# A decoder layer on one core: the layernorms' 16-bit rounded parts written by ACT instead of POOL

## The reference

```
x = x + attn(layernorm(x))           # 16 heads of 64, causal mask, w_qkv, w_out
x = x + xattn(layernorm(x), ctx)     # q, k from ctx (512 features); softmax(q k^T) mixes the features of x
x = x + ffn(layernorm(x))            # 8 experts: gate by score, best expert's low-rank update, bias
layernorm(x) = (x - mean(x)) / sqrt(var(x) + 1e-5)
```

## Time and profile before

| | us |
|---|---|
| median of 3 runs | 2772.9 (2771.0 to 2775.31) |
| the profiled execution, its own time | 2772.5 |
| its span in the trace | 2770.6 |
| PE busy | 2404.3 (87%) |
| DVE busy | 1884.6 (68%) |
| ACT busy | 782.0 (28%) |
| POOL busy | 717.5 (26%) |

### The profile page before, as it was taken

How to read it: one execution, slowest core, us unless ns; L and a number is a source line. 1 busy time by engine, 2 the same in 40 slices (tenths; PEclk the granted TensorE clock), 3 DMA queues, 4 the chain that set the end, 5 groups by cost and what they waited for, 6 DMA issues and landing times.

```text
span 2770.6 us, 37859 instructions
## 1 busy us (share of the span) xinstructions
PE 2404.3 (87%) x14389; PEld 1186.3 (43%) x14389; DVE 1884.6 (68%) x3421; ACT 782.0 (28%) x1557; POOL 717.5 (26%) x981
## 2 busy tenths in 40 slices
PE   0588888689898999869998999969989999986997
PEld 0233444344454444444444444434444444434544
DVE  4577887646876767755786777764696777764566
ACT  1033333321213333322212333431221333332110
POOL 3122433213402222212421222221330222221220
PEclk9899999899999999979999999989999999998997
DMA  6678787856746776775753777774773677776543
GB/s 177 216 174 182 161 214 179 189 140 145 146 108 126 141 151 135 140 181 129 147 125 100 150 139 143 146 186 109 158 147 106 117 149 146 143 154 159 107 76 91
DMA packets 986009, 403.97 MB, mean 146 GB/s; under 512 B 937116, under 2 KB 946332, under 8 KB 985828
## 3 DMA queue, kind: packets, MB, share of 16 engines
q1 hardware_dynamic: 985828, 401.56, 65.8%
HBM read 133.05 MB, written 33.55 MB: 60 GB/s over the span
## 4 chain that ended last, share of the span: by engine, by line
PE 59%; DVE 19%; DMA 10%; issue 6%; ACT 3%; POOL 2%; SPq 1%; ACTq 0%; POOLq 0%; DVEq 0%
PE ps_p L537 8%; PE ps_p L538 8%; PE ps_p L539 8%; DMA r<-pn 8%; PE ps_s L537 6%; PE ps_s L538 6%; PE ps_s L539 6%; PE ps_s L582 6%; PE ps_o L607 5%; DVE pn L816 4%; DVE peak L853 3%; ACT probs L742 2%; DVE bn L821 2%; DMA qk<-in_x 2%; PE ps_s L587 1%
## 5 line engine op out<-in xcount | busy, mean ns | idle before, releaser
L1080 POOL TENSOR_SCALAR pn<-probs,rden 128x640 f16<-128x640 f32 (+7 forms) x512 | 391.9, 778 | 1332.7 <-DVE rden L865 827.1
L742 ACT ACTIVATE probs<-ps_s,low,back 128x640 f32<-128x640 f32 (+7 forms) x512 | 421.7, 827 | 950.8 <-DVE low L856 840.1
L816 DVE SCALAR_TENSOR_TENSOR pn<-probs,rden,pn 128x640 f16<-128x640 f32 (+7 forms) x512 | 476.3, 962 | 193.1 <-POOL pn L1080 192.8
L537 PE MATMUL ps_p<-r,w 128*128 128x512 f16 x1344 | 515.1, 383 | 3.1 <-DVE qk L816 3.1
L538 PE MATMUL ps_p<-r,w 128*128 128x512 f16 x1344 | 514.2, 383 | 0.0
L539 PE MATMUL ps_p<-r,w 128*128 128x512 f16 x1344 | 513.7, 382 | 0.0
L582 PE MATMUL ps_s<-qk 64*128 64x512 f16 (+3 forms) x2304 | 239.0, 332 | 107.9 <-ACT probs L742 97.9
L853 DVE TENSOR_REDUCE peak<-ps_s 128x2 f32<-128x1280 f32 (+3 forms) x128 | 241.4, 1886 | 92.8 <-PE ps_s L587 90.3
L607 PE MATMUL ps_o<-r,vn 128*64 128x512 f16 (+3 forms) x2304 | 210.9, 339 | 39.3 <-issue 30.0
L539 PEld LDWEIGHTS ps_p<-r,w 128*128 128x128 f16 x1344 | 132.5, 99 | 162.1 <-issue 6.3
L582 PEld LDWEIGHTS ps_s<-qk 64*128 64x128 f16 x2304 | 90.0, 95 | 252.3 <-ACT probs L742 147.4
(11 more groups left out here) (167 smaller groups left out, 3554.0 us busy)
## 6 DMA issues: line engine op xcount, KB each, us to landing
w<-w_pairs SPq DMA_DIRECT2D x72, 512.0 KB, 4.0
qk<-in_x SPq DMA_DIRECT2D x32, 512.0 KB, 4.3
r<-wo_pairs SPq DMA_DIRECT2D x16, 1024.0 KB, 7.3
w_raw<-in_x SPq DMA_DIRECT2D x32, 512.0 KB, 4.6
out<-r SPq DMA_DIRECT2D x32, 512.0 KB, 2.9
r<-in_w_qkv SPq DMA_DIRECT2D x24, 512.0 KB, 5.8
w_raw<-in_w_qkv SPq DMA_DIRECT2D x24, 512.0 KB, 5.1
w_pairs<-w SPq DMA_DIRECT2D x24, 512.0 KB, 5.5
```

The source lines that it names most:

```text
L537: pe.matmul(ps, lh, rh, start=start and k == ks[0], stop=False)
L742: act.activation(probs_part(q, j, w), ps_s[:, j, scores(q)], ACT.Exp, bias=low[:, n % 2, i:i + 1], scale=sc, accum_out=den[:, n % 2, i:i + ...
L816: dve.scalar_tensor_tensor(out=to, in0=bank, scalar=scale, in1=rounded, op0=ALU.mult, op1=ALU.subtract).then_inc(ok, 1)
L1080: pool.tensor_scalar(to, src, scale, 1.0, ALU.mult, ALU.mult).then_inc(ok, 1)
```

## The change

The rounded part of each layernorm is no longer made by POOL from the fp32 row that ACT has written. ACT writes it itself, straight from x, by a second activation with the same scale and bias. The steps AH, LH and TH leave POOL's lists and enter ACT's: LH directly behind LX, TH behind TX, AH directly ahead of AX (which overwrites x). In each of the three layernorms that is 32 instructions, 96 in all. The waits for the buffers' release move along with them. What AX waits for is now the completion of AH, and DVE's AL waits for AX instead of AH.

```
 ACT_TAIL = """
...
-    QH3 LX0 OH1 CE0 LX1 CE1 CE2 CE3 LX2 CE4 CE5 CE6 CE7 AX0+ AX1+ AX2+ TX0 LX3 AX3+ TX1
...
+    LX0 LH0 OH1 CE0 LX1 LH1 CE1 CE2 CE3 LX2 LH2 CE4 CE5 CE6 CE7 AH0+ AX0+ AH1+ AX1+ AH2+ AX2+ TX0 TH0 LX3 LH3 AH3+
...
                     if kind == "AX":
-                        act.wait_ge(a_sh, T + 1)
+                        act.wait_ge(a_hi, T + 1)
...
+                    elif kind == "AH":
+                        act.wait_ge(a_sh, T + 1)
+                        if T >= 2:
+                            act.wait_ge(xt_in[T % 2], 16 * (T // 2))
...
+                    elif kind == "LH":
+                        if T > 0:
+                            act.wait_ge(t2_in, 16 * T)
+                        act.activation(xh2[:, 0, :], x1[:, i, :], ACT.Identity, bias=sh2[:, i:i + 1],
+                                       scale=rs2[:, i:i + 1]).then_inc(b_hi, 1)
+                    elif kind == "TH":
+                        if T > 0:
+                            act.wait_ge(t3_in, 16 * T)
+                        act.activation(xh3[:, 0, :], x1[:, i, :], ACT.Identity, bias=sh3[:, i:i + 1],
+                                       scale=rs3[:, i:i + 1]).then_inc(d_hi, 1)
...
                     elif kind == "AL":
-                        dve.wait_ge(a_hi, T + 1)
+                        dve.wait_ge(a_xn, T + 1)
```

More of the change, by code:

```diff
@@ L74 @@
 ACT_TAIL = """
-    E00 E01 CH21 E10 E11 E20 E21 KH E30 E31 JH0 OH1- E40 E41 QH0 JH1 E50 E51 OH0 E60 E61 QH1 JH2 E70 E71 QH2 JH3
-    QH3 LX0 OH1 CE0 LX1 CE1 CE2 CE3 LX2 CE4 CE5 CE6 CE7 AX0+ AX1+ AX2+ TX0 LX3 AX3+ TX1
-    LX4 AX4+ TX2 GE0 LX5 AX5+ TX3 GE1 WHI0 LX6 AX6+ TX4 GE2 WHI1 LX7 AX7+ TX5 GE3 WHI2 TX6 GE4 WHI3 TX7 GE5 WHI4
-    CH00+ CH01+ GE6 WHI5 CH10+ CH11+ GE7 WHI6 CH20+ WHI7 CH21+
+    E00 E01 CH21 E10 E11 E20 E21 KH E30 E31 JH0 OH1- E40 E41 QH0 JH1 E50 E51 OH0 E60 E61 QH1 JH2 E70 E71 QH2 JH3 QH3
+    LX0 LH0 OH1 CE0 LX1 LH1 CE1 CE2 CE3 LX2 LH2 CE4 CE5 CE6 CE7 AH0+ AX0+ AH1+ AX1+ AH2+ AX2+ TX0 TH0 LX3 LH3 AH3+
+    AX3+ TX1 TH1 LX4 LH4 AH4+ AX4+ TX2 TH2 GE0 LX5 LH5 AH5+ AX5+ TX3 TH3 GE1 WHI0 LX6 LH6 AH6+ AX6+ TX4 TH4 GE2 WHI1
+    LX7 LH7 AH7+ AX7+ TX5 TH5 GE3 WHI2 TX6 TH6 GE4 WHI3 TX7 TH7 GE5 WHI4 CH00+ CH01+ GE6 WHI5 CH10+ CH11+ GE7 WHI6
+    CH20+ WHI7 CH21+
 """
 POOL_TAIL = """
[L81 to L84, removed]
+    H00 H01 H10 H11 H20 H21 H30 H31 H40 H41 H50 H51 H60 H61 H70 H71 LS0 CHI0 LS1 CHI1 LS2 CHI2 CHI3 LS3
+    CHI4 CHI5 LS4 CHI6 LS5 CHI7 LS6 AS0+ AS1+ LS7
+    AS2+ TS0 AS3+ TS1 AS4+ TS2 AS5+ TS3 AS6+
+    TS4 AS7+ TS5 TS6 TS7
 """
@@ L102 @@
 ACT_START = """
-    AX0+ AX1+ AX2+ AX3+ AX4+ AX5+ AX6+ AX7+ CH00+ CH01+ CH10+ CH11+ CH20+ CH21+
+    AH0+ AX0+ AH1+ AX1+ AH2+ AX2+ AH3+ AX3+ AH4+ AX4+ AH5+ AX5+ AH6+ AX6+ AH7+ AX7+ CH00+ CH01+ CH10+ CH11+ CH20+
+    CH21+
 """
 POOL_START = """
-    AS0+ AS1+ AH0+ AH1+ AS2+ AH2+ AS3+ AH3+ AS4+ AH4+ AS5+ AH5+ AS6+ AH6+ AS7+ AH7+ WH0+ WH1+ WH2+ WH0++ WH1++
+    AS0+ AS1+ AS2+ AS3+ AS4+ AS5+ AS6+ AS7+ WH0+ WH1+ WH2+ WH0++ WH1++
 """
@@ L756, in rest @@
                     if kind == "AX":
-                        act.wait_ge(a_sh, T + 1)
+                        act.wait_ge(a_hi, T + 1)
                         act.activation(x_in[:, T % 2, :], x_in[:, T % 2, :], ACT.Identity, bias=sh1[:, i:i + 1],
                                        scale=rs1[:, i:i + 1]).then_inc(a_xn, 1)
+                    elif kind == "AH":
+                        act.wait_ge(a_sh, T + 1)
+                        if T >= 2:
+                            act.wait_ge(xt_in[T % 2], 16 * (T // 2))
+                        if i < 2 and b > 0:
+                            for s in range(2):
+                                act.wait_ge(at_in[s], 16 * 4 * b)
+                        act.activation(xh1[:, T % 2, 0, :], x_in[:, T % 2, :], ACT.Identity, bias=sh1[:, i:i + 1],
+                                       scale=rs1[:, i:i + 1]).then_inc(a_hi, 1)
+                    elif kind == "LH":
[8 more added lines that the diff above has]
+                                       scale=rs3[:, i:i + 1]).then_inc(d_hi, 1)
                     elif kind == "KH":
@@ L1119, in rest @@
                         sigma(T, mv1[:, i, :], ve1[:, i:i + 1], rs1[:, i:i + 1], sh1[:, i:i + 1], a_mv, a_ve, a_rs, a_sh)
[L1120 to L1127, removed]
                     elif kind == "VH":
@@ L1143, in rest @@
                         sigma(T, mv2[:, i, :], ve2[:, i:i + 1], rs2[:, i:i + 1], sh2[:, i:i + 1], b_mv, b_ve, b_rs, b_sh)
[L1144 to L1148, removed]
                     elif kind == "TS":
                         sigma(T, mv3[:, i, :], ve3[:, i:i + 1], rs3[:, i:i + 1], sh3[:, i:i + 1], d_mv, d_ve, d_rs, d_sh)
[L1151 to L1155, removed]
                 pool.memset(ones[:, :], 1.0)
```

## The result

| | kernel before | changed kernel |
|---|---|---|
| median us | 2772.9 (2771.0 to 2775.3) | 2790.4 (2788.6 to 2796.2) |
| ratio | | 1.0066, 95% interval 1.0049 to 1.0084 |
| profiled execution, own time / span | 2772.5 / 2770.6 | 2789.4 / 2787.6 |
| PE, DVE busy | 2404.3, 1884.6 | 2404.0, 1854.0 |
| ACT, POOL busy | 782.0, 717.5 | 893.5, 593.4 |

The account below looks back on a forecast made before the run. PE was taken as the bound in the scores stage, DVE in the FFN stage. 30.3 + 8.8 + 1.2 - 22.3 = +18.0 us on 2772.5 gave 2790.5 us, 0.6% slower; range 2779 to 2803.

Parts of the forecast that it names:

- N2 later, four tails: Scores stage: LH1 waits on ACT for LT0's landing, delaying CE1 and PE's N2 by 7.1 to 8.3 us; +30.3 us.
- clock behind the stalls: After each of four stalls ahead of N2, PE's lowered clock loses 2.2 us (1.4 to 3.0) of work; +8.8 us.
- gate, fourth tail: GE and WHI stand behind TH on ACT; one 1.14 us spacing passes through DVE to F6; +1.2 us.
- FFN stage, three tails: F0 to F5: DVE, relieved of POOL's company and waits, lets PE finish 7.4 us earlier a tail; -22.3 us.
- The second wait (LH2 for LT1): On ACT ahead of CE4: expected hidden and counted at nothing, 1 to 2 us a tail if a landing is slow.
- Rival 1: Ahead of N2: PE does not stall, leaving only the gain and the gate's 1.2; 2751 us, 12% chance.
- the collision excess: FFN stage: extra duration of DVE instructions while POOL rounds beside them, 10.6 us a tail, to go with the change.
- the bound of 10 to 13 us from PE's own need: F0 to F5: 76.6 us against five full-clock tiles, 66.5; PE can give back 10 to 13 us a tail at most.
- the walk: DVE's FFN account: 16.5 us saved, less 3.4 for TH and some 2.5 and 2 of new waits; F4 8.6 us earlier.
- its 2781: Total if each of 13 DVE-POOL collisions cost POOL's whole 1.05 us, winning up to 3 us more a tail.
- Rival 2: FFN stage: the stall comes but no gain, as ACT replaces POOL in holding up DVE; 2813 us, 13% chance.
- Rival 3: FFN stage: DVE stops being the bound, three tails give back PE's full 12.9 us each; 2774 us, 7% chance.

Follow-up runs that it names:

- Run 1: Changed kernel with LH1 placed behind CE2 on ACT instead of ahead of CE1; 2756.5 us, 0.9934 of the kernel before.
- Run 2: Changed kernel with transpose LT0 issued ahead of CT0 on SP, ACT's order untouched; 2750.7 us, 0.9917 of the kernel before.
- run 4: Changed kernel with TH behind GE and WHI on ACT from the third tile on, LT0's place unchanged; 2775.0 us, 1.0006 of the kernel before.
- run 6: Changed kernel with POOL writing unread stand-in copies at its old roundings' places, except TH's last two; 2813.8 us, 1.0136 of the kernel before.
- run 10: The fastest version with AH alone put back on POOL, in the tails and at the start; 2745.4 us, 0.9884 of the kernel before.
- the fastest version: Changed kernel with both LT0 ahead of CT0 on SP and TH behind GE and WHI on ACT; 2737.9 us, 0.9861 of the kernel before.
- run 3: Changed kernel with LH alone back on POOL in its old places, AH and TH staying on ACT; 2763.5 us, 0.9955 of the kernel before.

## Why the prediction held, step by step

The forecast of 2790.5 us stood against 2790.4, by the mechanism that it named. That the two agree to 0.1 us is luck: the terms were off by up to 2.9 us, in both directions, and mostly cancelled. (The ends of the stated range, 2779 and 2803, do not quite follow from its terms either: gains of 11 and 5 us a tail with the clock's 1.4 and 3.0 a stall give 2777 and 2801.)

| term | predicted | measured |
|---|---|---|
| N2 later, four tails | +30.3 | +28.3 (N1 to N2 13.64, 13.61, 13.70, 13.65 less 6.59) |
| clock behind the stalls | +8.8 | +6.9 (N2 to N3 8.46, 8.37, 8.47, 7.99 less 6.59) |
| gate, fourth tail | +1.2 | +1.4 (F6's wait +1.13, the rest behind it) |
| FFN stage, three tails | -22.3 | -19.4 |
| sum | +18.0 | +17.2 |

- **The stall.** Place, releaser and length held: ACT idle ahead of LH1, CE1 behind it, PE idle ahead of N2. I had read each tail's landing off its own LT0 and got 7.1 to 8.3 us; in the changed kernel LH1 starts 5.0 to 5.1 us after LT0's issue in every tail (before, POOL's 5.1 to 6.3), so all four are 7.0 to 7.1. That the idle engines leave the DMA less company there is a guess, not shown.
- **The clock.** In each tail the granted clock is at half level for 6.83 us, but this begins ahead of N2, so only the last 3.3 to 4.2 us of it fall on work: 1.4 to 1.9 us a stall instead of the 2.2 taken from other waits.
- **The second wait (LH2 for LT1) at nothing**: right for this kernel, with 1.2 to 1.7 us on ACT and none on PE. Run 1 shows the cover it had: the first stall. Without that it costs 0.4 to 0.9 us of gap in the three later tails.
- **Rival 1 (no stall)** needed a landing about 7 us earlier. Run 2 made it come early by SP's order and gave 2750.7 us, where the rival's sum was 2751.
- **The gate.** One spacing of 1.14 a tile held to 0.1 us in each wait (run 4). That TH ahead of WHI was worth 3.9 us a tail, near the 3.4 foreseen, is partly luck: only two of the three spacings reached PE (2.3 us), and the rest is clock (1.6), which this term did not hold.
- **The gain** is the term that was mis-sized: 6.5 us a tail instead of 7.4. Its cause, the collision excess, held (runs 6 and 10), and so did the bound of 10 to 13 us from PE's own need: freed of TH ahead of WHI, it is 10.3. The step that failed is the count of what stands against it: the walk left 12.0 us before the gate's 3.4. DVE's rows of the second tail, in the stretch of the earlier trace rows and the one 8.6 us later in the changed kernel, say where: its instructions are 10.6 us shorter and its waits for WHI 3.4 longer (4.5 instead of 1.1), both as counted; but of the 5.9 us of waits for vn and the load of x only 2.2 went (3.1 and 0.6 remain), against 2.1 of new waits for pn. So this part gives 0.1 us where the walk had 1.4, and DVE gains 7.3, not 8.6, of which PE gets 6.7 in that tail. WLO's wait of 1.5 us and the durations of 1.2 to 1.3 us came as written.
- **The rule on the shared port**, by the Trainium skill (SBUF — State Buffer, section SBUF: two separate sides): one of DVE and POOL has the port pair for its whole instruction and the other is blocked until then. Run 6's timelines agree: 0.22 us of work lasted 1.00, up to the end of POOL's instruction, and POOL's 1.04 lasted 1.99 behind DVE's. But what the blocked side pays is what is left of the other's instruction, 0.8 to 0.95 us in these rows. I had taken the rule to cost a full 1.05 a collision, hence its 2781; that was my reading of it and not what it says.
- **Rivals 2 and 3** fell: ACT did not take POOL's place (F0 to F5 6.5 us shorter), nor did DVE stop being waited for (two waits of 2.2 us a tail remain, two of 1.1 in the fastest version).

## What to carry to other kernels

Before an instruction moves to another engine, look at what it waits for: on the old engine the wait may have cost nothing, on the new one everything behind it in the queue inherits it, and here one landing waited for at the wrong place (35 us) ate the whole gain and more. Such a move brings its profit only with the orders around it: a transfer issued earlier and one instruction placed behind the small ones that others wait for turned +0.7% into -1.4%. And an engine off the critical path can slow the one on it by merely running beside it; the place to read that is the mean duration of the same instruction with and without company.

## What was unexpected of the hardware

- DVE and POOL block each other in turns, whichever started later (run 6): POOL's copy takes 1.04 us alone and up to 2.08, DVE's subtraction of two SBUF rows 1.22 and 2.05. ACT's six wide activations a tile, on the same rows, lengthened nothing: DVE's subtractions stay at 1.21 to 1.22 us.
- What a wait of PE does to its clock is not told by its length alone: two waits of 2.15 and 2.24 us, 16 us apart, were followed by 3.4 us at half clock (1.6 us of lost work), two of 1.02 and 1.11 by none. Run 2 had one of 2.14 us followed by 3.4 us at half clock as well; the same wait ahead of F2 in the changed kernel was followed by none within 10 us. In the third tail of run 3 even waits of 3.29 and 3.01 us were followed by none, in its first tail waits of 3.29 and 2.99 by 10.2 us. What decides there stays open.
